# A three-layer decoder kernel on one core: no transposes of the identity in TensorE's planned waits

## The chip, the cores and the metric

The kernel runs on one core of a Trainium2 chip. The metric is the device time of one execution, in microseconds. Its matrix engine is TensorE (PE in the rows; PEld is its weight load), beside VectorE (DVE), ScalarE (ACT), GpSimd (POOL) and SyncE (SP), which issues the transfers.

## The reference

The input x is 4 x 512 x 512 and a second input ctx is 4 x 512 x 256, in float32. Three residual layers follow each other:

```
x = x + attn(layernorm(x))            # 16 heads of 32, rotary, causal softmax, w_qkv, w_o
x = x + ssm(ctx, z=layernorm(x))      # in_proj, causal conv of 4 taps, silu, x_proj, dt_proj,
                                      # scan over 512 steps, 512 channels x 16 states, gate silu(z)
x = x + ffn(layernorm(x))             # bitlinear 512->2048, gelu, bitlinear 2048->512,
                                      # ternary weights, layer_norm before each
```

The scan is `state = state * exp(delta * A) + delta * u * B_t`, `y_t = sum_n state * C_t`, then `y + D * u`, times `silu(z)`.

## The kernel before

The work is cut into items. An item is a kind and its numbers, for example ("fc", t, n), and each engine has its share of it. The kinds that the prediction touches are, on TensorE: `ln1b`, the transposes of normalised x (line 1635); `inproj`, the input projection (1644); `xproj` (1653), `dt` (1669) and `ct` (1662); `rot`, the q and k projection (1679); `v` (1692); `s`, the scores (1703, 1707, 1711); `t`, the transposes of the softmax numerators (1722); `pv` (1734); `rz` (1771); `ht`, the transposes of the scan's states (1748), which VectorE then adds up (1847); `wo`, the output projection of attention (1760); `gt` (1778); `wtot` (1786); and in the feed-forward layer `fc` (1795, 32 matmuls per tile of 128 rows) and `proj` (1805, 32 matmuls per tile). VectorE does the convolution (1879) and the scans (1825, 1833); ScalarE does the exponentials of the scan (1415), of the softmax (1526) and the gelu (1587); GpSimd makes the scan's input (1295).

Batches are processed one after the other, and the layers overlap: the scan of batch b runs beside the attention of batch b + 1, and the last batch's scan beside the feed-forward tiles 0 to 13. Tiles 14 and 15 are alone at the end. The order on each engine is not written by hand. `schedule()` gives each item a due time, and `plan()` places the items one by one, with a table of estimated durations, and returns the order on each engine, the PSUM bank of each item that TensorE writes, and a third table, `fill`. An engine runs its items in that order, strictly, and waits on semaphores for its inputs.

The third table counts instructions that compute nothing. Where the planner expects TensorE to wait for an item's data after its PSUM bank is free, it enters a number of transposes of the identity matrix:

```
            fill[item] = int(FILL * max(0.0, at - max(room, free[engine])) / FILL_US)
```

`at` is the planned time of the item, `room` the planned time at which the bank is free, `free[engine]` the planned end of TensorE's item before. FILL_US, 0.11, stands for the time of one such transpose, and FILL is the part of the planned wait that is filled. TensorE's function `stand_by`, called ahead of each item, waits for the bank and then issues that many transposes into it; only after them does the item wait for its data. They are line 1622:

```
            def stand_by(*item):
                bank_free(*item)
                for _ in range(FILLS[item]):
                    nc.tensor.transpose(bank(*item)[:, 0:P], ident[:], ident[:])
```

The number is a constant of the program, so they run whether the data has come or not. What they write is overwritten by the item.

Of the kernel before, what the change touches and what calls it, by code (L numbers as in the profile page):

```python
# [396 lines left out]
READER = {**EMPTIED_BY, "gt": "dve", "wtot": "dve", "s": "dve", "t": "act", "fc": "act",  # L397
          "proj": "dve"}
DA_BANKS = (4, 5)
FILL, FILL_US = .5, 0.11  # L400


def reader_before(b, c):
# [1708 lines left out]
```

How the kernel before makes its waits and increments, by code:

```python
        def consts(eng, *groups):  # L1007
            for group in groups:
                eng.wait_ge(const_in[group], 16 * len(CONSTS[group]))
# [21 lines left out]
        def delta_made(eng, b, et):  # L1031
            if b == 0:
                eng.wait_ge(delta_ready["dve"], et + 1)
            else:
                eng.wait_ge(delta_ready["pool"], ET * (b - 1) + et + 1)
# [5 lines left out]
        def x_split(eng, t):  # L1042
            eng.wait_ge(x_lo[lo_by(t)], lo_turn(t))
# [1 line left out]
        def h_split(eng, t, n):  # L1046
            eng.wait_ge(h_lo[lo_by(t)], 2 * lo_turn(t) - 1 + n)
# [16 lines left out]
        def y_filled(eng, item):  # L1065
            eng.wait_ge(y_full, Y_TURN[item] + 1)
# [1 line left out]
        def y_taken(eng, item):  # L1069
            who, count = Y_FREED[item]
            eng.wait_ge(y_free[who], count)
# [5 lines left out]
        def hb_free(eng, e):  # L1078
            if e >= HB_RING:
                old = (e - HB_RING) // 2
                y_filled(eng, ("ht", old, blocks(old)[-1]))
                if 2 * BEGUN.get(old, 0) in CARRIED:
                    eng.wait_ge(carry_done, 2 * BEGUN[old] + e % 2 - LAST + 1)
# [1 line left out]
        def delta_over(eng, b):  # L1086
            eng.wait_ge(da_ready, 2 * DS * (b + 1))
# [6 lines left out]
        def emptied(eng, n):  # L1095
            who, count = FREED[n]
            eng.wait_ge(m_free[who], count)
# [1 line left out]
        def bank_free(*item):  # L1100
# [9 lines left out]
                y_taken(nc.tensor, user)  # L1110
            elif kind == "e":
                nc.tensor.wait_ge(e_done, 5 * a[0] + a[1] + 1)
            elif kind == "t":
                nc.tensor.wait_ge(p_ready, 5 * a[0] + a[1] + 1)
            elif kind == "scan":
```

## Time and profile before

| | |
|---|---|
| median of 3 runs | 1058.46 us (1055.85 to 1059.35) |
| the profiled execution's own time | 1058.11 us |
| its span, first to last instruction | 1056.3 us |
| mean granted TensorE clock in it | 0.969 |
| busy: TensorE / VectorE / ScalarE / GpSimd | 949.3 / 853.2 / 764.9 / 616.9 us |
| line 1622 | 612 instructions, 79.4 us busy |
| share of the chain that ended last | PE 57%, DVE 20%, issue 9%, ACT 7%, POOL 4%, DMA 2% |

A busy time of TensorE counts each instruction from its start to its modelled end, and neighbours overlap, so a row's mean is longer than the distance between two starts. The granted clock is 1.00 at 2.4 GHz and 0.50 at 1.2 GHz. The profile has no clock record before 10 us, and its views print 1.00 there.

### The profile page before, as it was taken

How to read it: one execution, taken by the hardware profiler on the slowest of the kernel's cores; microseconds unless marked ns; L12 is line 12 of the kernel's file. 1: busy time of each engine (PE TensorE's matmuls, PEld its weight loads, DVE VectorE, ACT ScalarE, POOL GpSimd, SP SyncE). 2: the span in 40 equal slices, each digit the busy share in tenths (PEclk: the TensorE clock that was granted, in tenths of full speed). 3: DMA queues.
4: the chain of work that ended last, by engine and by line, in shares of the span. 5: the costliest groups of instructions: out<-in, count | busy, mean ns of one | idle time of the engine just before them, and what ended most of it. 6: DMA issues, size and time to landing. Idle time of an engine off the chain costs nothing.

```text
span 1056.3 us, 18159 instructions
## 1 busy us (share of the span) xinstructions
PE 949.3 (90%) x5848; PEld 641.1 (61%) x5848; DVE 853.2 (81%) x1151; ACT 764.9 (72%) x1478; POOL 616.9 (58%) x439
## 2 busy tenths in 40 slices
PE   6989998899988999979889997667889999999997
PEld 5466666668755567765555876556755555555544
DVE  5797878986999987898999686998998889885431
ACT  4776867646787775677898669958279989996431
POOL 1387496555545778444658872345667768985410
PEclk9999999999999999978999998989989999999999
DMA  5356265265326544342336555224325565646553
GB/s 168 101 171 187 84 188 172 86 193 155 116 81 217 159 140 136 110 131 60 110 111 205 194 169 192 61 90 138 97 71 116 110 125 120 120 95 140 99 93 69
DMA packets 142812, 136.84 MB, mean 130 GB/s; under 512 B 92336, under 2 KB 96688, under 8 KB 141696
## 3 DMA queue, kind: packets, MB, share of 16 engines
q1 hardware_dynamic: 142720, 135.68, 46.1%
q8 instruction: 49, 0.80, 0.3%
q14 instruction: 43, 0.35, 0.1%
HBM read 90.42 MB, written 24.25 MB: 109 GB/s over the span
## 4 chain that ended last, share of the span: by engine, by line
PE 57%; DVE 20%; issue 9%; ACT 7%; POOL 4%; DMA 2%; SPq 0%; DVEq 0%; ACTq 0%; POOLq 0%
PE ps L1679 10%; PE ps L1748 8%; PE ps L1805 8%; PE ps L1795 8%; DVE hb L1825 6%; PE ps L1692 5%; PE ps L1760 5%; DVE y_acc L1847 4%; PE ps L1722 4%; DVE m_col L1922 2%; PE ps L1734 2%; POOL hb L1295 2%; ACT p_q L1526 2%; PE ps L1622 2%; DVE du L1879 1%
## 5 line engine op out<-in xcount | busy, mean ns | idle before, releaser
L1295 POOL TENSOR_TENSOR hb<-du,b_bc 128x1024 f32<-128x1024 f32 (+1 forms) x160 | 311.5, 1967 | 160.3 <-PE ps L1748 146.6
L1825 DVE TENSOR_TENSOR_SCAN hb<-ps,hb 128x1024 f32<-128x1024 f32 (+1 forms) x128 | 257.2, 2013 | 15.9 <-ACT ps L1415 13.5
L1415 ACT ACTIVATE ps<-delta,a_neg 128x511 f32<-128x511 f32 (+2 forms) x320 | 179.2, 597 | 72.6 <-DVE hb L1825 71.3
L1847 DVE SCALAR_TENSOR_TENSOR y_acc<-ps,ct,y_acc 128x512 f32<-128x512 f32 x256 | 182.0, 742 | 39.0 <-PE ps L1748 38.3
L1748 PE MATMUL ps<-ident,hb 128*128 128x128 f32 x1088 | 157.1, 288 | 35.1 <-DVE hb L1825 15.5
L1748 PEld LDWEIGHTS ps<-ident,hb 128*128 128x128 f32 x1088 | 129.5, 148 | 66.1 <-issue 17.8
L1526 ACT ACTIVATE p_q<-ps,m_col 128x512 f32<-128x512 f32 (+3 forms) x256 | 131.6, 530 | 26.4 <-DVE m_col L1922 22.0
L1795 PE MATMUL ps<-t_fc,xt 128*128 128x512 f16 x512 | 119.4, 387 | 3.3 <-DMA xt<-xs 3.3
L1679 PE MATMUL ps<-xn_t,w_ring 128*128 128x512 f32 x256 | 118.7, 608 | 2.2 <-DVE y_acc L1969 1.0
L1805 PE MATMUL ps<-t_pr,ht 128*128 128x512 f16 x512 | 114.7, 383 | 3.7 <-DMA ht<-hs 3.3
L1542 ACT ACTIVATE p_t<-ps 128x512 f32<-128x512 f32 x160 | 86.5, 603 | 30.6 <-PE ps L1722 30.2
L1722 PE MATMUL ps<-ident,p_q 128*128 128x128 f32 x640 | 89.2, 286 | 14.3 <-ACT p_q L1526 8.9
L1922 DVE TENSOR_REDUCE m_col<-ps 128x1 f32<-128x512 f32 (+2 forms) x192 | 88.0, 502 | 10.9 <-PE ps L1707 9.5
L1703 PE MATMUL ps<-k_st,q_st 128*128 128x512 f32 (+3 forms) x256 | 75.9, 373 | 19.5 <-DVE y_acc L1847 10.5
L1722 PEld LDWEIGHTS ps<-ident,p_q 128*128 128x128 f32 x640 | 76.2, 148 | 25.2 <-ACT p_q L1526 10.8
L1805 PEld LDWEIGHTS ps<-t_pr,ht 128*128 128x128 f16 x512 | 50.2, 99 | 64.3 <-issue 5.9
L1622 PE MATMUL ps<-ident 128*128 128x128 f32 x612 | 79.4, 279 | 8.8 <-DMA small<-in_small 5.9
L1795 PEld LDWEIGHTS ps<-t_fc,xt 128*128 128x128 f16 x512 | 50.7, 99 | 60.0 <-issue 4.5
L1679 PEld LDWEIGHTS ps<-xn_t,w_ring 128*128 128x128 f32 x256 | 47.5, 194 | 54.1 <-issue 50.6
L1622 PEld LDWEIGHTS ps<-ident 128*128 128x128 f32 x612 | 70.6, 144 | 15.4 <-DMA small<-in_small 5.9
L1056 POOL TENSOR_TENSOR hs<-h_sb,hs 128x1024 f16<-128x1024 f32 x28 | 60.6, 2170 | 21.4 <-ACT hs L1577 21.3
L1587 ACT ACTIVATE h_sb<-ps,gain 128x512 f32<-128x512 f32 x64 | 42.2, 685 | 36.9 <-PE ps L1795 36.5
(141 smaller groups left out, 1559.5 us busy)
## 6 DMA issues: line engine op xcount, KB each, us to landing
w_ring<-in_w_attn SPq DMA_DIRECT2D x32, 512.0 KB, 3.7
qk_d<-hl SPq DMA_DIRECT2D x64, 256.0 KB
q_st<-qk_d SPq DMA_DIRECT2D x128, 128.0 KB, 2.9
b_bc<-bc_d SPq DMA_DIRECT2D x48, 256.0 KB, 3.7
k_st<-qk_d SPq DMA_DIRECT2D x64, 128.0 KB, 2.7
k_st<-qk_d SPq DMA_DIRECT2D x128, 64.0 KB, 2.3
x_in<-in_x SPq DMA_DIRECT2D x16, 256.0 KB, 2.8
raw_fc<-in_w_fc SPq DMA_DIRECT2D x4, 1024.0 KB, 9.5
```

Of the source, the lines that this page charges most:

```text
L1295: nc.gpsimd.tensor_tensor(piece_of(e, hi, lo).rearrange("p (a n) -> p a n", a=2), du[b % 2][:, 2 * h:2 * h + 2, lo:hi], b_bc[:, i % BC_RIN ...
L1415: ins = nc.scalar.activation(factors(j, hi, lo)[:, (hi - lo) * m + start:(hi - lo) * (m + 1)], delta[b % 2][:, et, lo + start:hi], ACT.Exp ...
L1526: ins = nc.scalar.activation(p_q[:, h, Q_AT[i]:Q_AT[i] + w], src[:, col:col + w], ACT.Exp, bias=m_col[:, i, h:h + 1], accum_out=z_sum[:, b ...
L1622: nc.tensor.transpose(bank(*item)[:, 0:P], ident[:], ident[:])
L1679: mm = nc.tensor.matmul(bank(kind, *a), w_ring[:, c % 2, d, P * half:P * half + P], xn_t[:, d, :], start=(d == 0), stop=(d == KD - 1))
L1722: mm = nc.tensor.transpose(dst[:, at:at + P], p_q[:, h, Q_AT[i] + P * jt:Q_AT[i] + P * jt + P], ident[:])
L1748: mm = nc.tensor.transpose(bank(kind, *a)[:, P * et:P * et + P], piece_of(2 * r + et // 2, hi, lo)[:, at:at + P], ident[:])
L1795: mm = nc.tensor.matmul(bank(kind, t, n), xt[:, t % 2, KD * m + d, :], t_fc[:, d, 512 * n:512 * n + 512], start=(d == 0 and m == 0), stop= ...
L1805: mm = nc.tensor.matmul(bank(kind, t), ht[t % 2][:, k // 8, 8 * m + k % 8, :], t_pr[:, pr_row(k), :], start=(k == 0 and m == 0), stop=(k = ...
L1825: v.tensor_tensor_scan(h, d, h, 0.0, ALU.mult, ALU.add).then_inc(scan_done, 1)
L1847: v.scalar_tensor_tensor(out=y, in0=bank(kind, r, tb), scalar=ct[:, b % 2, tb, n:n + 1], in1=y, op0=ALU.mult, op1=ALU.add).then_inc(y_free ...
L1922: ins = v.tensor_reduce(m_col[:, i, h:h + 1], src[:, col:col + P * (i + 1)], AX.X, ALU.max, negate=True)
```

## The change

One number: the part of each planned wait that is filled is 0 instead of one half. The planner's decisions do not depend on the table of fills.

```diff
-FILL, FILL_US = .5, 0.11
+FILL, FILL_US = 0, 0.11
```

TensorE's first instructions, from the program's start: the transposes of the identity (ident alone), the transposes of x (x_in), the input projection (in_w) and the x projection (xp_w), before:

```order
1 L1622 MATMUL ps<-ident 128x128 x33
2 L1635 MATMUL ps<-ident,x_in 128x128 x4
3 L1622 MATMUL ps<-ident 128x128 x2
4 L1635 MATMUL ps<-ident,x_in 128x128 x4
5 L1622 MATMUL ps<-ident 128x128
6 L1644 MATMUL ps<-ctx_in,in_w 128x512 x8
7 L1622 MATMUL ps<-ident 128x128 x31
8 L1653 MATMUL ps<-du_100,xp_w 48x512 x4
```

and what stands there now:

```order
1 L1635 MATMUL ps<-ident,x_in 128x128 x8
2 L1644 MATMUL ps<-ctx_in,in_w 128x512 x8
3 L1653 MATMUL ps<-du_100,xp_w 48x512 x4
4 L1635 MATMUL ps<-ident,x_in 128x128 x8
5 L1669 MATMUL ps<-x_dbl,dt_w 128x512 x2
```

The 33 and the 2 ahead of the first eight transposes of x are gone, and so are the 1 after them and the 31 after the input projection; the rest stands in its order.

TensorE's last instructions, feed-forward tiles (fc with t_fc, proj with t_pr and the transposed h), as one piece of the difference:

```order
 L1805 MATMUL ps<-t_pr,ht_121 128x512 x32
 L1795 MATMUL ps<-t_fc,xt 128x512 x8
-L1622 MATMUL ps<-ident 128x128 x37
 L1805 MATMUL ps<-t_pr,ht_120 128x512 x32
 L1795 MATMUL ps<-t_fc,xt 128x512 x32
 L1805 MATMUL ps<-t_pr,ht_121 128x512 x32
 L1795 MATMUL ps<-t_fc,xt 128x512 x32
-L1622 MATMUL ps<-ident 128x128 x22
 L1805 MATMUL ps<-t_pr,ht_120 128x512 x32
-L1622 MATMUL ps<-ident 128x128 x28
 L1805 MATMUL ps<-t_pr,ht_121 128x512 x32
```

Three groups ahead of projections are gone and nothing else has moved. In all 612 instructions in some sixty groups go; VectorE, ScalarE, GpSimd and SyncE have the same programs as before.

## Rows read from the trace of the kernel before

**Rows 1.** The page: TensorE's busy time; granted clock in 40 slices.

```profile
PE 949.3 (90%) x5848; PEld 641.1 (61%) x5848; DVE 853.2 (81%) x1151; ACT 764.9 (72%) x1478; POOL 616.9 (58%) x439
...
PEclk9999999999999999978999998989989999999999
```

**Rows 2.** Windows: length, busy of PE, PEld, DVE, ACT, POOL, clock, DMA, GB/s.

```profile
30.00:66.00 36.00, 36.00 (x130) 20.23 (x129) 31.06 (x44) 30.49 (x44) 21.60 (x15) 1.00 0.38 129
...
120.00:210.00 90.00, 80.71 (x542) 57.77 (x541) 78.14 (x104) 62.74 (x148) 62.18 (x38) 0.98 0.45 137
...
630.00:700.00 70.00, 48.45 (x415) 40.43 (x412) 60.11 (x73) 58.21 (x121) 23.53 (x11) 0.90 0.35 120
...
738.00:767.00 29.00, 23.76 (x152) 21.11 (x151) 28.65 (x37) 6.99 (x17) 16.83 (x13) 1.00 0.37 106
...
797.00:884.00 87.00, 84.20 (x454) 45.81 (x452) 73.25 (x108) 80.80 (x131) 66.93 (x66) 1.00 0.57 116
884.00:984.00 100.00, 98.75 (x524) 52.73 (x522) 73.75 (x123) 83.43 (x114) 70.14 (x67) 1.00 0.59 120
```

**Rows 3.** The instructions of line 1622: duration in ns min/median/max.

```profile
L1622 PE MATMUL ps<-ident x612: 272/273/474, 5.9 to 1041.9; 128*128 128x128 f32 x153
```

**Rows 4.** Windows for line 1622 alone: length, PE, PEld, clock, DMA, GB/s.

```profile
5.80:9.90 4.10, 4.02 (x19) 4.03 (x20) 1.00 0.50 197
10.00:11.60 1.60, 1.60 (x15) 1.44 (x14) 1.00 0.00 0
...
797.00:884.00 87.00, 3.86 (x30) 3.53 (x31) 1.00 0.57 116
```

**Rows 5.** The chain that ended last, 0 to 30 us: start, us, what.

```profile
5.88 5.80 PE ps L1622 x33
...
12.14 2.65 DMA x_in<-in_x
...
16.04 0.67 DVE du L1879
...
25.65 3.63 PE ps L1653 x8
```

**Rows 6.** Timeline of VectorE: start, us, instruction.

```profile
5.54 0.54 DVE L1863 TENSOR_SCALAR x_in<-x_in,mv,rstd 128x512 f32<-128x512 f32 x1
```

**Rows 7.** Timeline of SyncE's queue, 2 to 5 us.

```profile
3.07 0.43 SPq L1155 DMA_DIRECT2D in_w<-in_in_w x1
```

**Rows 8.** Transfers of the first 60 us: KB each, us to landing.

```profile
in_w<-in_in_w SPq DMA_DIRECT2D x1, 512.0 KB, 5.3
```

**Rows 9.** The chain from 30 us on: pieces of line 1622.

```profile
53.83 0.77 PE ps L1622 x7
...
738.71 2.51 PE ps L1622 x23
...
961.37 0.11 PE ps L1622
```

**Rows 10.** Timeline of TensorE; in brackets idle time before, and what ended it.

```profile
19.59 3.55 PE L1622 MATMUL ps<-ident 128*128 128x128 f32 x31
...
200.66 2.46 PE L1622 MATMUL ps<-ident 128*128 128x128 f32 x21
204.71 0.66 PE L1722 MATMUL ps<-ident,p_q 128*128 128x128 f32 x4 [1.60 <-ACT p_q L1526]
...
996.72 4.20 PE L1622 MATMUL ps<-ident 128*128 128x128 f32 x37
1001.98 7.07 PE L1805 MATMUL ps<-t_pr,ht 128*128 128x512 f16 x32 [1.06 <-DMA ht<-hs]
...
1044.34 8.68 PE L1805 MATMUL ps<-t_pr,ht 128*128 128x512 f16 x32 [2.21 <-DMA ht<-hs]
```

**Rows 11.** Windows of all engines where the granted clock is 0.50.

```profile
1044.30:1047.60 3.30, 3.26 (x8) 1.19 (x9) 0.00 (x0) 0.00 (x0) 0.00 (x0) 0.50 0.00 0
460.60:467.30 6.70, 6.09 (x25) 5.32 (x26) 6.61 (x11) 5.04 (x16) 0.80 (x2) 0.50 0.57 168
```

## The prediction

> **What bounds the kernel now.** I began with the page's shares: TensorE is busy for 90% of the span, and the clock line shows how often its granted clock dips [rows 1]. A 90% engine looks like the bound, but some of that share is the work under question, so I went on to the table by stretch [rows 2]. Read each row as busy time against length. From 30 to 66 us TensorE has no pause at all. From 120 to 210 us TensorE (80.7 of 90) and VectorE (78.1) share the work and hand the path to one another. From 738 to 767 us VectorE is busy 28.65 of 29.00 us: it is the bound there, whatever TensorE does. From 797 to 884 us ScalarE has 80.8 of 87; from 884 to 984 us TensorE has 98.8 of 100. Then I asked for the transposes of the identity alone (line 1622, called fillers below): 612 of them, 273 ns each as recorded; they overlap, so what one occupies is its pitch [rows 3]. The windows for that line show the pitch at both clocks: 19 in 4.10 us at the start (0.21 us each), then 15 in 1.60 us (0.11 us each) [rows 4]. So the fillers occupy 612 x 0.11 = 67 us of TensorE. Most stand where TensorE would wait anyway; the question is which do not, and what the rest buy.
>
> **What the change takes away, and what that gives.** Only the 612 fillers go. TensorE's remaining instructions keep their order, and the other engines' programs are the same. Nothing moves past a queue.
>
> The start. TensorE begins 33 fillers at 5.88 us, and the chain runs through them for 5.80 us, then through the first transposes of x, then through the load of the third x tile, 2.65 us from 12.14 us [rows 5]. But VectorE had the first x tile ready at 5.54 + 0.54 = 6.1 us [rows 6]. Without fillers its four transposes run at the slow pitch (4 x 0.21 = 0.9 us) and are done near 7.2 us, so the load of the third tile starts about 5 us earlier. The next thing late is the input projection: its weights are issued at 3.07 us and take 5.3 us, so it can begin at 8.4 us [rows 7, 8]. Its first output needs four matmuls, each 0.45 us at 2.4 GHz (eight of the same width take 3.63 us in [rows 5]) and double at 1.2 GHz: 1.8 to 3.4 us, then a ScalarE pass of somewhat under 1 us. The convolution on VectorE, which starts at 16.04 us now, starts at 11.7 to 12.7 us. Gain 3.3 to 4.3 us; I take 3.8. It carries on, since after 25.65 us TensorE is without a pause up to 66 us and needs nothing that lands later than the x tiles.
>
> Fillers on the chain further on. Followed through the whole span, the chain holds seventeen more pieces of line 1622, together 9.3 us: the first at 53.83 us, the last at 961.37 us, the largest 2.51 us at 738.71 us; seven of them lie from 833 us on (3.3 us) and nine lie up to 210 us (3.5 us) [rows 9]. On these TensorE had its data and still ran fillers. Those from 833 us lie where TensorE is the bound: all 3.3 us come back. Of the nine early ones I take all 3.5. The 2.51 us piece stands where VectorE is full [rows 2]: 0.5 us. Beside the chain, 797 to 884 us holds 30 fillers in all [rows 4], of which the chain has eleven; the other 19 (2.1 us) I count at nothing, because ScalarE's 80.8 us of work [rows 2] covers them. If that cover is not there they are 2.1 us more. The 22 fillers just before the last two projections cost nothing now either: the last projection waits for a transfer at 1044.3 us in any case [rows 10].
> Gains: 3.8 + 3.5 + 0.5 + 3.3 = 11.1 us.
>
> **What the change takes away besides.** The fillers keep the granted clock up. The evidence is in [rows 4]: between 5.8 and 11.6 us TensorE executes nothing but fillers, and the pitch drops from 0.21 to 0.11 us, that is from 1.2 to 2.4 GHz. The Trainium skill, "TensorE: Matmul & The Clock Gate", Part 4 (PE-mode transpose), says that work in transpose mode does not count as busy for the clock. By that rule the fillers would hold no clock, and removing them would cost nothing: the sum would be minus 11.1 us. The trace speaks against it.
>
> What a lost clock costs is read at the end: the last projection starts at 1044.34 us after a wait, takes 8.68 us where the same 32 matmuls take 7.07 us, and the window 1044.3 to 1047.6 us shows 0.50 [rows 10, 11]. So an episode that ends after one such stretch costs 1.6 us. The upper bound comes from 460.6 to 467.3 us, where the clock stays at 0.50 for the whole 6.7 us [rows 11]: 3.35 us. TensorE resumes at an arbitrary moment, so I take 2.2 us, nearer the lower end.
>
> Which waits become episodes? The pattern is a wait partly filled: 21 fillers from 200.66 us, then a pause, next work at 204.71 us; 31 fillers from 19.59 us before work at 25.65 us; 37 from 996.72 us before work at 1001.98 us [rows 5, 10]. At present the clock survives them. Without fillers TensorE is idle for 4.1, 6.1 and 5.3 us. With a wait near 650 us these are the four waits over 4 us that lose a clock held now. After those at 25.65 and 1001.98 us TensorE is the path: 2 x 2.2 = 4.4. After 204.71 us matmuls of the q and k projection follow directly but VectorE shares the path: 1.6. Near 650 us TensorE is the least loaded of the three (48 of 70 us against 60 of VectorE and 58 of ScalarE [rows 2]): 0.8. Together 6.8 us.
> Seven shorter waits (2.2 to 3.3 us, near 68, 102, 162, 670, 707, 737 and 886 us) may or may not lower it: 7 x 0.6 x 2.2, half of it covered by VectorE, is 4.6 us.
> Five waits (near 77, 719, 767, 784 and 1044 us) are already followed by half clock; longer idleness adds perhaps 0.3 us each, 1.5 us.
> Losses: 6.8 + 4.6 + 1.5 = 12.9 us.
>
> Sum: 12.9 - 11.1 = 1.8 us slower. Against the profiled execution this is a span of 1056.3 + 1.8 = 1058.1 us and a time of 1058.11 + 1.8 = 1059.9 us; that execution lies 0.35 us under the median of the runs (1058.46), so against the median 1060.
>
> **The rivals.**
> 1. The clock loss dominates. If every episode lasts two stretches (3.35 us) and eight in ten of the shorter waits become one, the losses are 3.35 x (1 + 1 + 0.7 + 0.4) = 10.4, 7 x 0.8 x 3.35 x 0.5 = 9.4 and 1.5, 21.3 us in all, and the time is 1058.5 + 21.3 - 11.1 = 1068.7 us. For it: after the removal TensorE's waits are wholly empty, and short bursts between them do not obviously restore the clock (the 6.7 us stretch). Against: VectorE is nearly full in several of the places. It decides from an average episode of about 2.6 us on. With its milder forms chance 0.34, typical time 1065.
> 2. The returned time dominates. If episodes end after one stretch (1.6 us) and the shorter waits keep the clock, the losses are 1.6 x 3.1 + 1 = 6.0 us and the time is 1058.5 - 11.1 + 6.0 = 1053.4 us. For it: the seventeen chain pieces are seen, the episodes are not. Chance 0.19.
> 3. The fillers hold no clock, so only the gains are left: 1058.5 - 11.1 = 1047.4 us. Against it stands the pitch that halves under fillers alone. The page named above is what would give this. Chance 0.07.
> 4. Both effects cancel, my forecast: chance 0.40.
>
> **How the numbers follow.** The measurement tells about 0.3% (3.2 us) from no change. My case gives 1055.3 to 1061.6 us, with 1060 as its value. Slower by more takes rival 1, 0.34; faster by more takes rivals 2 and 3, 0.26; same 0.40. For eight times in ten the range must hold rival 2's 1053.4 and most of rival 1; I leave out rival 3's end and the last of rival 1: 1051 to 1068 us. With all gains at their upper bounds (2.0 and 2.1 us more) and the losses of rival 2 the time would be 1049.3 us, just outside.
>
> **What the next profile would show.** Line 1622 gone. The projection of inputs starting near 8.4 us and the convolution starting near 12 us instead of 16.04 us (if not, the start's 3.8 us fail). Half clock under the x projection at about 22 us and under the matmuls that now start at 1001.98 us, whose 32 take 9 us or more instead of 7.07 us (if they keep 7.07, the clock argument fails and rival 2 or 3 holds). The mean granted clock falling from 0.969 to about 0.93 to 0.95. From 884 to 984 us about 2 us less. The prediction is wrong if the start's gain does not reach 66 us, or if one part (episodes of 3.35 us in full, or ScalarE's cover missing) is mis-sized by more than 3 us.

## The result, and the profile after

The kernel without the transposes is slower: 1069.57 us (1066.65 to 1072.96, five runs) against 1059.17 us (1055.85 to 1060.19, five runs of the kernel before on the same chip), a ratio of 1.0103 with a 95% interval of 1.0071 to 1.0136. The forecast was 1060 us with a range of 1051 to 1068 us. The median lies outside the range, on the side of rival 1. The profiled execution's span is 1067.7 us (1056.3 us before) and its mean granted clock 0.933 (0.969).

The page of the kernel after, to be read against [rows 1]: busy times, the granted clock in 40 slices, and the chain that ended last.

```profile
PE 910.5 (85%) x5236; PEld 590.1 (55%) x5236; DVE 854.2 (80%) x1151; ACT 765.4 (72%) x1478; POOL 615.3 (58%) x439
...
PEclk9988998999999999978999997878988999999898
...
PE 55%; DVE 21%; issue 10%; ACT 7%; POOL 5%; DMA 1%; SPq 0%; DVEq 0%; ACTq 0%; POOLq 0%
```

612 instructions and 38.8 us of busy time have gone from TensorE. That is less than the 67 us that the transposes occupied, because what is left runs longer at the lower clock. The other engines' work is unchanged. The clock line has new or deeper dips at the start (slices 3, 4 and 7), from about 640 us on (slices 25 to 31), and near the end (slices 38 and 40).

Windows of the kernel after, in the stretches of [rows 2], with the same columns.

```profile
30.00:66.00 36.00, 36.00 (x129) 20.11 (x130) 31.18 (x44) 31.24 (x45) 21.78 (x15) 1.00 0.43 129
120.00:210.00 90.00, 75.72 (x475) 53.12 (x475) 77.90 (x105) 62.42 (x147) 64.33 (x39) 0.94 0.45 131
630.00:700.00 70.00, 48.03 (x384) 38.76 (x376) 59.43 (x80) 59.91 (x122) 26.43 (x13) 0.83 0.39 129
738.00:767.00 29.00, 20.73 (x126) 16.43 (x118) 28.34 (x35) 10.80 (x26) 15.53 (x14) 1.00 0.37 119
797.00:884.00 87.00, 79.46 (x404) 41.59 (x403) 72.63 (x103) 78.38 (x127) 65.11 (x63) 0.96 0.53 114
884.00:984.00 100.00, 96.37 (x493) 50.05 (x492) 78.50 (x132) 91.00 (x124) 75.24 (x74) 0.98 0.60 117
```

From 630 to 700 us TensorE holds 31 instructions fewer than in [rows 2] and is busy as long as before: the clock went from 0.90 to 0.83. From 797 to 884 us it went from 1.00 to 0.96, and TensorE, which had 84.2 us of 87, has 79.5.

Where the time went, by matching the same instruction in the two traces. The number is how much later (in us) the kernel after starts it.

```
at us in before      7     26     30     66    100    160    205    212    640
later by          -5.35  -1.23  +0.67  -0.09  +2.11  +1.78  +4.15  +5.74  +4.34

at us in before    672    720    741    794    797    812    883    980   1005
later by          +5.70  +6.90  +3.62  +6.11  +3.49  +8.60  +8.43  +8.98 +11.01
```

One trace is one execution, and runs of one kernel differ by about 3 us, so this shows places, not prices. The start's gain is used up at 30 us. Then the loss comes in steps: near 100, from 160 to 212, near 812, and at the last projections.

Each step has its half clock. Windows of the kernel after where the clock stands at 0.50 over the whole length:

```profile
93.60:100.30 6.70, 6.70 (x25) 4.77 (x23) 3.43 (x3) 3.01 (x7) 4.75 (x3) 0.50 0.94 263
165.30:172.00 6.70, 6.07 (x28) 5.60 (x27) 5.85 (x12) 4.58 (x11) 6.70 (x4) 0.50 0.82 192
806.90:813.70 6.80, 5.08 (x16) 2.91 (x17) 5.36 (x7) 6.77 (x12) 5.46 (x6) 0.50 0.53 101
1008.40:1015.10 6.70, 4.17 (x10) 1.49 (x11) 0.00 (x0) 4.26 (x4) 3.16 (x4) 0.50 0.70 132
1052.70:1059.50 6.80, 4.17 (x10) 1.50 (x11) 0.00 (x0) 0.00 (x0) 0.00 (x0) 0.50 0.42 99
```

Note the lengths. Inside its span the kernel before has 15 stretches of half clock in its trace, four of them 6.8 us long and eleven 3.4 us, 64.6 us together. The kernel after has 26, and 16 of them are 6.8 us long, 142.8 us together. I write **half-clock time** below for 2 x (1 - mean clock) x span, the mean over all runs of a kernel: 62 us before (43 runs), 143 us after (five runs). It leaves out the start: the trace's clock record begins at 10.0 us in the kernel before, at 15.0 us in the kernel after and at 13.9 us in e7_nostart, and until then the views print 1.00. In the window 10 to 15 us of the kernel after they do so over seven matmuls that fill the 5.00 us, where the x projection's eight of the same width take 3.63 us at 2.4 GHz.

TensorE's timeline in the kernel after, at the places of [rows 10]:

```profile
6.17 2.02 PE L1635 MATMUL ps<-ident,x_in 128*128 128x128 f32 x8 [6.17 <-DVE x_in L1863]
8.98 10.11 PE L1644 MATMUL ps<-ctx_in,in_w 128*128 128x512 f32 x16 [0.80 <-DMA in_w<-in_in_w]
24.04 5.91 PE L1653 MATMUL ps<-du,xp_w 128*48 128x512 f32 x8 [4.95 <-issue]
...
1010.93 9.13 PE L1805 MATMUL ps<-t_pr,ht 128*128 128x512 f16 x32 [5.07 <-DMA ht<-hs]
1042.79 7.07 PE L1805 MATMUL ps<-t_pr,ht 128*128 128x512 f16 x32 [2.01 <-DMA ht<-hs]
1055.33 8.90 PE L1805 MATMUL ps<-t_pr,ht 128*128 128x512 f16 x31 [5.47 <-DMA ht<-hs]
```

(A matmul of the program in fp32 stands in these rows as two, so the input projection's eight are x16.) The x projection starts 1.6 us earlier than before and takes 5.91 us instead of 3.63. The projection that took 7.07 us after 37 transposes takes 9.13 us after an empty wait of 5.07 us. In the middle row a wait of 2.01 us did not bring the clock down.

### The profile page after: what moved, and what is told of

It reads as the page before. It is cut to its first block, busy times and chain, and to the rows that moved or that the text cites. A ratio compares the mean times of both kernels' runs of the same rounds, so it can differ in the third digit from the quotient of the medians.

```text
span 1067.7 us, 16969 instructions
## 1 busy us (share of the span) xinstructions
PE 910.5 (85%) x5236; PEld 590.1 (55%) x5236; DVE 854.2 (80%) x1151; ACT 765.4 (72%) x1478; POOL 615.3 (58%) x439
## 4 chain that ended last, share of the span: by engine, by line
PE 55%; DVE 21%; issue 10%; ACT 7%; POOL 5%; DMA 1%; SPq 0%; DVEq 0%; ACTq 0%; POOLq 0%
PE ps L1748 8%; PE ps L1805 8%; PE ps L1679 8%; PE ps L1795 7%; DVE hb L1825 7%; PE ps L1722 5%; PE ps L1692 5%; PE ps L1760 4%; DVE y_acc L1847 4%; DVE m_col L1922 2%; PE ps L1734 2%; POOL hb L1295 2%; PE ps L1644 2%; ACT p_q L1526 2%; PE ps L1669 1%
## 5 line engine op out<-in xcount | busy, mean ns | idle before, releaser
L1825 DVE TENSOR_TENSOR_SCAN hb<-ps,hb 128x1024 f32<-128x1024 f32 (+1 forms) x128 | 257.2, 2013 | 15.4 <-ACT ps L1415 13.5
L1748 PE MATMUL ps<-ident,hb 128*128 128x128 f32 x1088 | 162.0, 295 | 53.2 <-DVE hb L1825 31.0
L1748 PEld LDWEIGHTS ps<-ident,hb 128*128 128x128 f32 x1088 | 133.6, 152 | 86.1 <-issue 44.2
L1795 PE MATMUL ps<-t_fc,xt 128*128 128x512 f16 x512 | 121.8, 393 | 7.7 <-issue 7.7
L1805 PE MATMUL ps<-t_pr,ht 128*128 128x512 f16 x512 | 117.2, 389 | 13.0 <-DMA ht<-hs 12.6
L1722 PE MATMUL ps<-ident,p_q 128*128 128x128 f32 x640 | 96.6, 303 | 24.6 <-ACT p_q L1526 20.4
L1722 PEld LDWEIGHTS ps<-ident,p_q 128*128 128x128 f32 x640 | 83.1, 158 | 37.3 <-issue 15.6
L1703 PEld LDWEIGHTS ps<-k_st,q_st 128*128 128x128 f32 x256 | 44.9, 204 | 35.1 <-DVE y_acc L1847 14.2
L1760 PE MATMUL ps<-w_ring,o_t 128*128 128x256 f32 x256 | 58.6, 382 | 2.4 <-DVE xr_last L1945 2.3
```

The source lines that it names most:

```text
L1703: nc.tensor.matmul(dst[:, col:col + w], q_st[:, p % 2, h, P * i:P * i + P], k_st[:, p % 2, h, 0:w], start=(u == 0), stop=False)
L1722: mm = nc.tensor.transpose(dst[:, at:at + P], p_q[:, h, Q_AT[i] + P * jt:Q_AT[i] + P * jt + P], ident[:])
L1748: mm = nc.tensor.transpose(bank(kind, *a)[:, P * et:P * et + P], piece_of(2 * r + et // 2, hi, lo)[:, at:at + P], ident[:])
L1795: mm = nc.tensor.matmul(bank(kind, t, n), xt[:, t % 2, KD * m + d, :], t_fc[:, d, 512 * n:512 * n + 512], start=(d == 0 and m == 0), stop= ...
L1805: mm = nc.tensor.matmul(bank(kind, t), ht[t % 2][:, k // 8, 8 * m + k % 8, :], t_pr[:, pr_row(k), :], start=(k == 0 and m == 0), stop=(k = ...
L1825: v.tensor_tensor_scan(h, d, h, 0.0, ALU.mult, ALU.add).then_inc(scan_done, 1)
```

## The experiments

Three theories stood; the expectations call them A, B and C. A: half clock is the whole loss, and its episodes are longer and more than forecast. B: the loss is at the start, where the gain did not last. C: the gain is missing because a transpose ahead of work whose data was ready only moves a wait. A fourth, D, is that the clock does not matter and only the later start of TensorE's items helps. A changed table FILLS stands right behind the lines in which `plan()` makes ORDER, PLACE and FILLS; a changed `nc.tensor` line is the one in `stand_by`. No experiment changes what the kernel computes; only what runs in TensorE's waits differs. "Before" is the kernel before, in runs beside it: 1058.45 us (17 runs) for the first four experiments, 1059.11 us (15) for e5 to e8, 1057.58 us (11) for the others.

**e1_start: the start as it was, everything else removed.**

```diff
+START = {("ln1b", 0, 0), ("ln1b", 0, 1), ("inproj", 0, 0), ("xproj", 0)}
+FILLS = {x: n if x in START else 0 for x, n in FILLS.items()}
```

> Fillers kept only in the first four groups (33, 2, 1 and 31 instructions, up to the x projection of batch 0), 545 removed. Theory A (the loss is a sum of episodes of half clock all over the span, less the time given back): the start is worth what the two traces differ by at 30 us, 0.7 us, so this kernel is 9 to 11 us slower than before, 1067 to 1070 us, and shows the same half-clock stretches after 60 us as the changed kernel. Theory B (the start is the main loss, because the input projection and the x projection run at half clock there and everything behind them starts late): most of the 10 us come back, 1060 to 1062 us.

Measured: 1070.71 us, ratio 1.0117 [1.0093, 1.0140], half-clock time 137 us. Putting the start's 67 transposes back does not win anything; theory B falls.

**e2_waits: only the 181 transposes ahead of work that was ready removed.** 431 stay in the waits.

```diff
+READY = {"rot", "v", "wo", "s", "pv", "dt"}
+FILLS = {x: 0 if x[0] in READY or x[0] == "fc" and x[1] or x in (("proj", 9), ("proj", 14)) else n for x, n in FILLS.items()}
```

> 181 of 612 fillers removed: all those behind which TensorE's data was ready in the trace of before (ahead of rot, v, wo, s, pv, dt, of fc except the first tile's, and of the projections of tiles 9 and 14). The 431 in front of real waits stay. Theory A with separate terms (fillers on ready work are pure delay, fillers in waits hold the clock): faster than before by the chain pieces, 3 to 9 us, 1050 to 1056 us. Theory C (a wait is not removed with its filler: where the filler goes, the wait comes later, unfilled, and the clock falls there, as behind the 24 fillers at 794 us): no gain, 1057 to 1062 us, with half clock under the work near 805 us and 745 us that ran at full clock before.

Measured: 1060.26 us, ratio 1.0014 [1.0000, 1.0029], half-clock time 83 us. On balance these transposes cost nothing where they stood, although fifteen of the chain's seventeen pieces, 8.3 us of 9.3, are among them. Theory C had expected 1057 to 1062 us. The half-clock time rose by 21 us, so the balance is of two effects: some time came back, and some clock was lost. TensorE's timeline of e2_waits near 800 us shows both in one place. Before, 24 transposes stood here, at 794.04 us, ahead of 16 matmuls of `fc`:

```profile
795.33 0.60 PE L1748 MATMUL ps<-ident,hb 128*128 128x128 f32 x4
795.77 3.62 PE L1795 MATMUL ps<-t_fc,xt 128*128 128x512 f16 x16
804.23 1.94 PE L1748 MATMUL ps<-ident,hb 128*128 128x128 f32 x8 [4.85 <-DVE hb L1825]
805.97 3.62 PE L1795 MATMUL ps<-t_fc,xt 128*128 128x512 f16 x8
```

The 16 matmuls come sooner, and then TensorE waits for VectorE's scan, 4.85 us instead of 2.25. The 2.6 us of the transposes are waited for in full. Now the wait is long and empty in one piece, the clock falls, and the next 8 matmuls take 3.62 us instead of 1.89. The kernel after has the same, at 808.62 us.

**e3_narrow: the transposes replaced by fp32 matmuls of 4 columns**, half as many again, to hold TensorE for the time with little work in its array.

```diff
+FILLS = {x: 3 * n // 2 for x, n in FILLS.items()}
-                    nc.tensor.transpose(bank(*item)[:, 0:P], ident[:], ident[:])
+                    nc.tensor.matmul(bank(*item)[:, 0:4], ones[:], ident[:, 0:4], start=True, stop=True)
```

> The fillers stand where they stood, half as many again (898), but each is a matmul of 4 columns in place of a transpose of 128, so TensorE's queue is held for a similar time with little work in the array. Theory A (it is the array's activity in the waits that holds the clock): half clock as in the changed kernel or more, and the delays of before on top, 1070 to 1080 us, granted clock 0.92 to 0.94. Theory D (what matters is that TensorE's next item starts later, not the clock): as before, 1056 to 1062 us.

Measured: 1281.99 us, ratio 1.2113, half-clock time 328 us. The size was missed: each is recorded as two passes, and the timeline of e3_narrow shows their pitch.

```profile
5.99 21.07 PE L1622 MATMUL ps<-ident,ones 128*128 128x4 f32 x98 [5.99 <-DMA small<-in_small]
26.91 1.09 PE L1635 MATMUL ps<-ident,x_in 128*128 128x128 f32 x4
```

98 passes in 21.07 us are 0.215 us each, 0.43 us for one matmul. 898 of them are some 386 us where the transposes occupied 67, nearly six times too much. The total says nothing about the theories. The rows do: for 21 us TensorE executed these back to back, and the four transposes behind them still took 1.09 us, which is the time at 1.2 GHz (0.60 at 2.4 GHz).

**e4_full: the whole planned wait filled.** 1272 transposes.

```diff
-FILL, FILL_US = .5, 0.11
+FILL, FILL_US = 1, 0.11
```

> FILL 1 in place of one half: 1272 fillers, the whole planned wait. Theory A: the granted clock rises to 0.98 or more, worth up to 3 us against before; the fillers on ready work double, and by the chain pieces that costs 5 to 9 us: 1060 to 1066 us. If the delay hardly matters (Theory C, the waits only move) the kernel is at 1054 to 1059 us.

Measured: 1077.20 us, ratio 1.0167 [1.0138, 1.0196], half-clock time 37 us, far above both values expected. The clock is nearly whole and the kernel is slower than both. Line 1622 is 12% of its chain (2% before), so real work now waits behind transposes, and that costs more than the clock gives. No run shows in which places.

**e5_short: as many instructions, each a quarter as long.** 612 f16 matmuls of 4 columns.

```diff
-                    nc.tensor.transpose(bank(*item)[:, 0:P], ident[:], ident[:])
+                    nc.tensor.matmul(bank(*item)[:, 0:4], ident[:].bitcast(F16)[:, 0:P], ident[:].bitcast(F16)[:, 0:4], start=True, stop=True)
```

> The 612 fillers stand where they stood, each now one matmul of 4 columns with 128 columns of float16 weights in place of a transpose of 128 columns. If one takes about the 0.11 us of a transpose, TensorE's items are held back as before, and only the array's work in the waits is gone. Theory A (the array's work holds the clock, and the clock is the whole cost): half-clock time as in the changed kernel, 130 to 150 us, nothing given back, so slower than the changed kernel: 1072 to 1082 us. What it is over before is then the clock's cost, and what it is over the changed kernel is the time that removing the fillers gives back. Theory D (the later start of TensorE's items is what helps): 1056 to 1062 us whatever the clock does.

Measured: 1067.04 us, ratio 1.0080 [1.0054, 1.0107], half-clock time 140 us. 33 of them take 1.04 us at the start, so their pitch is near 0.03 us. The expected 1072 to 1082 us supposed instructions as long as a transpose. The kernel behaves as the kernel after: 612 instructions this short in the waits hold no clock.

**e6_moved: the 181 of e2_waits removed and 328 put into waits for data**, where e2_waits' trace shows them, for example 42 ahead of the 8 transposes above, behind the 16 matmuls.

```diff
+READY = {"rot", "v", "wo", "s", "pv", "dt"}; MORE = {('xproj', 0): 21, ('ht', 2, 0): 18,
...
+FILLS = {x: (0 if x[0] in READY or x[0] == "fc" and x[1] or x in (("proj", 9), ("proj", 14)) else n) + MORE.get(x, 0) for x, n in FILLS.items()}
```

> The fillers on ready work are gone as in e2_waits, and 328 more stand in waits for data that the trace of e2_waits shows idle (42 ahead of the scan block at 803 us, where e2_waits ran at half clock). Theory A: half-clock time falls from 83 us in e2_waits to 40 to 60 us, at about 0.3 us of time each 8 to 12 us under e2_waits: 1050 to 1053 us, faster than before. Theory C in its strong form (what is saved on ready work is always waited for again): 1055 to 1059 us, not faster than before by more than the clock gives.

Measured: 1054.46 us, ratio 0.9948 [0.9928, 0.9967], half-clock time 47 us. TensorE's timeline of e6_moved at the same place:

```profile
793.44 3.62 PE L1795 MATMUL ps<-t_fc,xt 128*128 128x512 f16 x16
796.89 4.75 PE L1622 MATMUL ps<-ident 128*128 128x128 f32 x42
801.84 1.09 PE L1748 MATMUL ps<-ident,hb 128*128 128x128 f32 x8 [0.20 <-DVE hb L1825]
802.77 1.89 PE L1795 MATMUL ps<-t_fc,xt 128*128 128x512 f16 x8
```

The same wait is filled to within 0.20 us, the clock stays, and the 8 matmuls are back at 1.89 us. The time lies between what theory A (1050 to 1053 us) and theory C (1055 to 1059 us) gave.

**e7_nostart: only the start's 67 removed.** Its START is that of e1_start.

```diff
+FILLS = {x: 0 if x in START else n for x, n in FILLS.items()}
```

> Only the 67 fillers of the start (up to the x projection of batch 0) are removed, the other 545 stay. Theory A by the two traces: 0.7 us slower at 30 us, and so at the end, 1059 us; the prediction's step (3.8 us gained, 2.2 lost) would give 1057 us; Theory B (the start is the main loss) 1066 us or more.

Measured: 1055.60 us (ten runs), ratio 0.9972 [0.9956, 0.9988], half-clock time 61 us. TensorE's timeline of e7_nostart:

```profile
9.60 9.24 PE L1644 MATMUL ps<-ctx_in,in_w 128*128 128x512 f32 x16 [1.14 <-DMA in_w<-in_in_w]
23.95 5.30 PE L1653 MATMUL ps<-du,xp_w 128*48 128x512 f32 x8 [5.12 <-issue]
```

The start's gain is real and its clock loss too: 16 matmuls take 9.24 us where they took 7.03, and the x projection 5.30 us instead of 3.63. Net of both the start returns 3.0 us (0.28% of 1059), more than either value expected. The half-clock time leaves out the input projection's part of the loss, since the clock record of e7_nostart begins only at 13.9 us.

**e8_more: all 612 kept and 292 added in waits for data.**

```diff
+MORE = {('xproj', 0): 20, ('ht', 2, 0): 18, ('t', 4, 0): 9, ('ht', 8, 0): 5, ('rz', 2): 18, ('t', 7, 0): 12,
...
+FILLS = {x: n + MORE.get(x, 0) for x, n in FILLS.items()}
```

> All 612 fillers stay, and 292 more stand in the waits for data that the trace of before shows idle. No ready item is delayed more than before. Theory A: half-clock time falls from 63 us to about 40 us, 5 to 7 us faster, 1052 to 1054 us; against e6_moved it shows what the 181 fillers on ready work cost when the clock is held. If filling waits to the end delays the items behind them, 1059 us or more.

Measured: 1052.89 us, ratio 0.9941 [0.9920, 0.9961], half-clock time 39 us. It has 904 transposes where e6_moved has 759: the 181 ahead of ready work stay, and 36 fewer are added in waits. It is 1.6 us faster than e6_moved with 8 us less of half clock; the intervals of the two ratios overlap widely. Beside an otherwise held clock, having the 181 or not makes no difference that can be told.

**e9_held: TensorE held as long as before, without transposes.** Four of e5_short's matmuls for each transpose, 2448 in all, 0.11 us for each four.

```diff
+FILLS = {x: 4 * n for x, n in FILLS.items()}
-                    nc.tensor.transpose(bank(*item)[:, 0:P], ident[:], ident[:])
+                    nc.tensor.matmul(bank(*item)[:, 0:4], ident[:].bitcast(F16)[:, 0:P], ident[:].bitcast(F16)[:, 0:4], start=True, stop=True)
```

> In e5_short one narrow matmul took 0.027 us, a quarter of a filler's 0.109, so the queue was hardly held. Here there are four for each filler (2448), 0.108 us together: TensorE's items are held as long as before, with little work in the array. Theory A: half-clock time as in the changed kernel or more, 140 to 160 us; the time above before is the clock's whole cost, by 0.25 to 0.39 us for each of the 80 to 95 us more at half clock 20 to 35 us, so 1078 to 1093 us, and the part above the changed kernel (9 to 24 us) is what removing the fillers gives back. If the fillers' delay hardly matters (the waits only move): 1068 to 1073 us, like the changed kernel. Theory D (the delay helps, the clock doesn't matter): 1056 to 1062 us.

Measured: 1077.62 us, ratio 1.0180 [1.0153, 1.0207], half-clock time 146 us. This is the run that separates the two effects: TensorE's queue is held nearly as in the kernel before, the clock is that of the kernel after. TensorE's timeline of e9_held, at the start and at the projection of [rows 10] that had 37 transposes ahead of it:

```profile
5.30 3.68 PE L1622 MATMUL ps<-ident 128*128 128x4 f16 x132 [5.30 <-DMA small<-in_small]
8.85 1.09 PE L1635 MATMUL ps<-ident,x_in 128*128 128x128 f32 x4
...
1013.33 3.84 PE L1622 MATMUL ps<-ident 128*128 128x4 f16 x148
1019.55 9.43 PE L1805 MATMUL ps<-t_pr,ht 128*128 128x512 f16 x32 [2.37 <-DMA ht<-hs]
```

148 of them fill the wait nearly as 37 transposes did (3.84 us against 4.20), and the projection takes 9.43 us, not 7.07. At the start the transposes of x behind 132 of them take 1.09 us, the time at 1.2 GHz; behind the 33 transposes, 5.8 us of them, they took 0.60. (Here the queue was held for 3.7 us only, so this place by itself proves less than the 21 us of e3_narrow.) If their queue time costs what the transposes' did, the whole price of the clock is 0.0180 x 1058.5 = 19.1 us. The kernel after is 10.9 us slower than before (0.0103 x 1058.5), so the removal itself gave back 19.1 - 10.9 = 8.2 us, give or take some 4 us by the intervals of the two ratios. Both are estimates that rest on that condition. The kernel after lost 143 us to half clock and this one 146, near enough to take one for the other.

**e10_best: e8_more without the start's first 36**, with e8_more's MORE.

```diff
+FILLS = {x: 0 if x[0] in ("ln1b", "inproj") and x[1] == 0 else n + MORE.get(x, 0) for x, n in FILLS.items()}
```

> e8_more without the 36 fillers ahead of the first transposes and the first input projection; those ahead of the x projection (31 and 20 more) stay. By e7_nostart (3.5 us faster without the start's fillers) and e8_more (6.2 us faster), if they add: 1048 to 1050 us. If the gains overlap (a start at half clock ahead of the same path): 1052 to 1054 us.

Measured: 1046.28 us (1044.52 to 1053.77), ratio 0.9907 [0.9877, 0.9937], half-clock time 35 us. It is faster than both kernels, and faster than the 1048 to 1050 us expected if the two gains add. TensorE's timeline of e10_best (its profiled execution was the slowest of its six):

```profile
8.98 9.19 PE L1644 MATMUL ps<-ctx_in,in_w 128*128 128x512 f32 x16 [0.59 <-DMA in_w<-in_in_w]
18.00 5.73 PE L1622 MATMUL ps<-ident 128*128 128x128 f32 x51
23.66 3.63 PE L1653 MATMUL ps<-du,xp_w 128*48 128x512 f32 x8
```

The input projection starts at 8.98 us, as in the kernel after, at low clock. The 51 transposes in the wait that the gain opened then keep the x projection at 3.63 us.

**e11_ready: the complement of e2_waits.** The 181 ahead of ready work and the start's 67 stay; the 364 in the other waits go. READY and START as above.

```diff
+FILLS = {x: n if x[0] in READY or x[0] == "fc" and x[1] or x in (("proj", 9), ("proj", 14)) or x in START else 0 for x, n in FILLS.items()}
```

> The complement of e2_waits: the 181 fillers on ready work and the 67 of the start stay, the 364 in waits are gone. Theory A with the cost all in the waits: e2_waits was 0 to 3 us slower than before, so this one carries 10 to 13 us, 1069 to 1072 us, with half-clock time 120 to 135 us. If the 181 fillers on ready work also shorten the waits behind them, some of the clock is held: 1064 to 1068 us.

Measured: 1071.05 us, ratio 1.0128 [1.0103, 1.0153], half-clock time 128 us. The three parts add up: e2_waits +1.5, e7_nostart -3.0, e11_ready +13.5 (each its ratio less 1, times 1058.5) make +12.0, where all three together measured +10.9. The loss is in the waits for data, from 30 us on.

**e12_long: only the forecast's four long waits filled.** 137 transposes: 31 ahead of the x projection, 21 at 200 us, 35 and 13 near 650 us, 37 near 997 us.

```diff
+LONG = {("xproj", 0), ("t", 7, 0), ("wtot", 0), ("pv", 13), ("proj", 12)}
+FILLS = {x: n if x in LONG else 0 for x, n in FILLS.items()}
```

> Only five groups stay, 137 fillers: ahead of the first x projection (31), near 204 us (21), near 650 us (35 and 13) and near 1000 us (37): the four long waits of the prediction. By its prices they are worth 6.8 us of 12.9: 1062 to 1064 us against the changed kernel's 1069.6. If the loss lies mainly in the many shorter waits, 1066 to 1069 us.

Measured: 1064.96 us, ratio 1.0071 [1.0049, 1.0094], half-clock time 122 us. It lies between the two ranges expected. TensorE's timeline of e12_long:

```profile
1002.57 4.20 PE L1622 MATMUL ps<-ident 128*128 128x128 f32 x37
1007.82 7.07 PE L1805 MATMUL ps<-t_pr,ht 128*128 128x512 f16 x32 [1.05 <-DMA ht<-hs]
```

The 37 transposes by themselves bring this projection back from 9.13 to 7.07 us. But all 137 recover only 0.0103 - 0.0071, about 3.4 us, and 143 - 122 = 21 us of half clock; the intervals of the two ratios overlap, so this is a size and not a proof. It is also net of whatever delay the 137 cause. The other waits hold the larger part.

## Why the prediction was wrong

**What held.** Line 1622 gone and no other engine's work changed. The clock argument: the projection at 1001.98 us was to take 9 us or more and took 9.13; the mean clock was to be 0.93 to 0.95 and is 0.933 (the 39 us of half clock in the prediction's own sum, worked out below, would have given 0.951, so this range and the sum did not belong together); half clock lies under the x projection. 738 to 767 us is VectorE's: the instructions at 735 and 758 us are both 6.06 us later. From 30 to 66 us the kernel after makes up 0.76 us, the seven transposes of the chain piece at 53.83 us. The signs of both large terms were right, and rival 1 was named with its mechanism.

**The step that failed: how much half clock the removal brings.** The term is "Losses: 12.9 us", put together from episodes of 2.2 us, "nearer the lower end", because "TensorE resumes at an arbitrary moment". At half a microsecond of time for each microsecond at half clock, as the prediction reads its two ends, 2.2 us is an episode of 4.4 us. The trace of the kernel after shows 142.8 us of half clock against 64.6, so 78 us more. The prediction's own parts, turned into half clock in the same way, make 39 us:

| part | forecast, us of half clock | in the two traces, us |
|---|---|---|
| four long waits | 4 x 4.4 = 17.6 | 23.8: all four fall, three of them for 6.8 us |
| seven shorter waits | 7 x 0.6 x 4.4 = 18.5 | 30.6: six of seven fall, three of them for 6.8 us |
| five at half clock already | 5 x 0.6 = 3.0 | 13.6: four of them go from 3.4 to 6.8 us |
| places not in the list | 0 | 13.6 at 93.6 and 806.9 us, and 3.4 less near 334 us |

So episodes were more than forecast, and longer: 16 of 26 last 6.8 us, where only 4 of 15 did. Of the two places outside the list, the one at 806.9 us was made by the removal: a wait that transposes ahead of ready work had cut short became one empty wait. The fall at 93.6 us follows waits of 0.50, 0.24 and 0.80 us, and the kernel before has the same three, to within 0.03 us, and keeps its clock; no run shows why.

The price of a microsecond was put too high, which hides half of the error. The forecast has 12.9 us for 39 us, 0.33 us each. By e9_held the losses are 19.1 us for 84 us (146 - 62), 0.23 us each. That is less than the 0.5 us it would cost if TensorE alone set the end, presumably since elsewhere VectorE and ScalarE cover it. The four long waits show it best: their half clock was more than forecast, and filling them again (e12_long) brought back about 3.4 us, net, where 6.8 were put.

Rival 1 named this mechanism, and its 1068.7 us is close to the 1069.57 measured. That closeness is partly luck: its losses of 21.3 us are 2.2 above the 19.1 of e9_held, and its gains of 11.1 us are 2.9 above the 8.2. Its turning point, an episode of about 2.6 us (by the prediction's own weights 2.5), is passed: the 26 stretches last 5.5 us on average, 2.7 us in the prediction's count.

**The second step that failed: transposes on the chain come back in full.** The gains were put at 11.1 us and e9_held leaves 8.2. For the chain's pieces the prediction said "TensorE had its data and still ran fillers", "all 3.3 us come back". Of the fifteen pieces that e2_waits removes, among 181 transposes, the prediction wanted 6.3 us back (8.3 us, with 0.5 for the piece of 2.51). The kernel became 1.5 us slower [0.0, 3.1] with 21 us more of half clock; at 0.23 us each that is 4.8 us, so by this estimate 3.3 us came back, about half. What the earlier work gains is in part waited for a little later, for VectorE or for a transfer. From 884 to 984 us "about 2 us less" was expected; between 883 and 980 us the kernel after loses 0.55 us. Two things stand there in its trace: 3.4 us of half clock from 895.7 us, and longer waits for VectorE's scan (line 1833), 3.6 us where the kernel before waits 1.2. TensorE's waits from 884 to 984 us, kernel after:

```profile
PE ps L1748 <- DVE hb L1833: 3.6, 2, 2.7
```

The sentence that those pieces lie where TensorE is the bound was read from a share of 98.75 of 100 us. That share contained 30 of the transposes themselves, 3.3 us at their pitch; but even the 95 us that are left look like a bound, so it was not the share alone that misled. A share does not tell for what the engine will wait once it gets there sooner.

**The start.** The forecast was 3.8 us less 2.2 for the x projection's clock, 1.6 us net. e7_nostart measured 3.0 us net, over ten runs. The steps behind it were less good: the input projection did start at 8.98 us (8.4 forecast) and the first transposes 5.35 us sooner, but its matmuls, sixteen in the rows, ran at half clock for longer than the four I counted (10.11 us against 7.03). VectorE's timeline shows the convolution at 13.58 us, not at 11.7 to 12.7, so 2.5 us earlier than before and not 3.3 to 4.3.

```profile
13.58 2.32 DVE L1879 SCALAR_TENSOR_TENSOR du<-ps,small,du 128x511 f32<-128x511 f32 x3 [2.29 <-ACT du L1463]
```

In this one trace nothing of it is left at 30 us, which the runs of e7_nostart do not bear out as a mean.

**Rival 3**, that transposes hold no clock, is excluded. The Trainium skill, "TensorE: Matmul & The Clock Gate", Part 4 (PE-mode transpose), has them as not busy for the clock. This case disagrees: 33 of them, with nothing else on TensorE, raise it within 5.8 us [rows 4], and replacing all 612 by matmuls of 4 columns that hold TensorE nearly as long costs 1.8%.

**Left open.** Which of the smaller waits pays how much: no run takes them one by one. Why the clock falls at 93.6 us. And where e10_best's 6.6 us against e8_more go (0.9907 against 0.9941 is 3.6 us by the ratios, and e7_nostart explains 3.0 of it); the rest is within the spread of the runs, and the kernel before ran 1.5 us faster beside e10_best (1057.58 us) than beside e8_more (1059.11).

## What to carry to other kernels

An engine's busy share includes work that computes nothing: before calling an engine the bound of a stretch, take such work out of the share, and then ask for what the engine would wait if it came sooner. To price lost clock, count how long it is lost as well as how often; here the length was where much of the error lay. Filler work on TensorE pays by where it stands: in a wait for data whose length the trace shows it buys clock (e8_more, e10_best), ahead of work that is ready 181 transposes bought as much clock as they cost time (e2_waits), and filled to the planned wait in full it delays real work for more than the clock is worth (e4_full). When two effects of one edit have opposite signs, run a kernel that has only one of them, as e9_held does; the difference of two large terms can't be priced from the sum.

## What the runs showed of the hardware

Occupation of TensorE's queue by itself did not raise the granted clock. Matmuls of 4 columns left it at 1.2 GHz after 21 us in fp32 (e3_narrow) and after 3.7 us in f16 (e9_held), where 33 transposes of 128 x 128 raised it within 5.8 us. An fp32 matmul of 4 columns is recorded as two passes of about 0.215 us, at the start of e3_narrow; an f16 one has a pitch of 3.68 / 132 = 0.028 us at the start of e9_held and 3.84 / 148 = 0.026 us at 1013 us, where the granted clock is 1.00. A transpose, in contrast, halves its pitch with the clock [rows 4].

The runs of the kernel before spread by 0.65% (1054.2 to 1061.1 us), and most of that goes with the clock: over its 43 runs, time and half-clock time correlate at 0.84, with 0.25 us of time for one us of half clock. Runs with a mean clock of 0.974 or more take 1055.6 us on average, those of 0.967 or less 1060.5 us. For the kernel after the correlation is 0.99, with 0.39 us for one us, but from five runs only.
